# A pause in the token scatter at every fourth token tile

## The chip, the cores and the metric

One core of a Trainium2 chip runs the whole kernel. The metric is the device time of one execution in microseconds, as the median of the runs that were timed; smaller is better. The engines are named as the profile names them: PE is the matmul engine (PEld its weight loads), DVE the vector engine, ACT the scalar engine, POOL GpSimd, SP the engine that only issues transfers here.

## What is computed

The input is two sequences of 2048 tokens with 256 features. Both branches start from the layer-normed tokens. One is a spiking attention, the other a mixture of eight experts of which each token uses two. The reference, cut to this:

```python
xn = _layernorm(x)
# attention: Q, K, V are 0/1 spikes
Q = lif(layer_norm(query @ Wq.T + bq, gq, betaq), 1.0)      # K and V alike
hamming = q_sum + k_sum.T - 2.0 * qk
attn = Dh - hamming + log_pe_bias(N, N)
out = lif(einsum(attn * scale, V), 0.5)
out = lif(layer_norm(out @ Wo.T + bo, go, betao), 1.0)
# experts: each token goes to its two best of 8
scores, expert_idx = jax.lax.top_k(softmax(xt @ router_w.T), 2)
hidden = silu(h[..., :D]) * h[..., D:]                       # h = xt @ up_proj[e]
out_e = hidden @ down_proj[e]
result = x + attention + sum of the two out_e, weighted by gate
```

## The kernel before, in words

The 4096 tokens are 32 token tiles of 128. The normed tokens lie in SBUF as `xn`, 258 words a token: 256 features and two words that say where the expert result belongs. The program has these stages, in the order of time:

- **Start and routing** (0 to 65 us of the profile): load, norm, transposes, router logits, and on DVE the choice of experts. It ends with `pos`, two slot numbers for each token (semaphore `placed`, L901).
- **Scatter** (POOL, L677): `slot_x` is a DRAM buffer in which the tokens lie sorted by expert. For each of the 32 token tiles POOL issues two indirect transfers (TOPK = 2), each of which writes 128 rows of 1032 bytes to `slot_x`. That makes 64 transfers. Seven more (L684) write the empty slots; they are issued behind the tiles 3 to 6, two, two, two and one. POOL does not wait between them. Each of the 64 raises the semaphore `scattered` by 16 when it has landed.
- **Projection** (PE, ACT and DVE, beside the scatter): for each token tile PE computes Q, K and V. One tile is three groups of a bias matmul and six float32 matmuls (L1186, L1108 to L1110), and around them the transpose of an earlier tile's Q spikes (`turn_q`, L1174) and its K-V sum (`sum_kv`, L1195). ACT squares the results (`squares`, L500, waits for `proj_done`), moves Q (`keep_qT`, L488), and splits the next tile (`keep_xh`, L447); DVE makes the spikes (L960). The three engines hand tiles to each other in a short ring of buffers, so each is at most a few tiles ahead. Tiles 0 to 7 are written out, 8 to 19 are a loop, the rest is written out again. Tile 8 is the first of the loop; its project begins at 167.02 us in the profile, the last tile's ends at about 235 us.
- **Experts** (237 to 430 us): 71 slot tiles of 128 rows. SP reads them from `slot_x` (L353); before the first it waits for the whole scatter, for the seven others, and for the last expert weights that DVE splits. POOL writes each result with one indirect transfer to `slot_y` (L692).
- **Attention and output** (430 us to the end).

Who needs the scatter: SP's first read of `slot_x`, and nobody else. ACT waits at tile 11 for the seven other transfers (`pads_done`), since expert weights go where their rows lay.

Of the kernel before, what the change touches and what calls it, by code (L numbers as in the profile page):

```python
# [24 lines left out]
TOPK = 2  # L25
# [22 lines left out]
PAD_TILE = 3  # L48
LAG = 3
LATE = 11  # L50
FAR_ROWS = 5


# [4 lines left out]
def expert_blocks(a):  # L58

    n = [min(max(k - LAG, 0) * 4 // 3, NB) for k in (a, a + 1)]  # L60
    return range(*n)


def spiking_moe(nc, x, w_all, router, bias, gain, beta, scale, experts, ident, ident_b, toep, far_map, far_pick,
                head_mask, before, route_const, pad_mark, out):
    with ExitStack() as ctx:
        def sem(name):
            return ctx.enter_context(nc.semaphore(name))
# [177 lines left out]
        s = {n: sem(n) for n in names}  # L246
# [60 lines left out]
        def piece(n, h):  # L307
            return ew[:, n, h, :] if num(n) else ew[:, bass.ds(n, 1), h, :].rearrange("p a w -> p (a w)")

        def loop(eng, n, unroll, body, peel):  # L310

            for t in range(peel):
                body(t, t)
            with eng.Fori(0, (n - peel) // unroll) as i:
                for u in range(unroll):
                    body(i * unroll + (peel + u), peel + u)
# [8 lines left out]
        def _(sp):  # L325
# [57 lines left out]
            for a in range(NB):  # L383
                if a < LATE:
                    sp.wait_ge(s["fin_done"], a + 1)
                else:
                    sp.wait_ge(s["late_done"], a - LATE + 1)
                sp.dma_start(out_pairs[:, a], xres[:, a * B:(a + 1) * B, :]).then_inc(s["out_done"], 16)
# [237 lines left out]
        @block.gpsimd  # L626
        def _(pool):
            g = nc.gpsimd
            order = [0]

            def step(ins):
                order[0] += 1
                ins.then_inc(s["pool_order"], 1)

            def settled():
                pool.wait_ge(s["pool_order"], order[0])

            step(g.memset(neg_half[:, :], -0.5))
            g.memset(ones_b[:, :], 1.0).then_inc(s["ones_set"], 1)
            step(g.memset(pad_rows[:, :, :], 0.0))  # L640
            step(g.memset(ones_r[:, :].bitcast(F32), 1.0))
            step(g.memset(far_v[:, :], 0.0))
            g.memset(eps_c[:, :], EPS).then_inc(s["eps_set"], 1)
            step(g.memset(half_s[:, :], 0.0))
            step(g.memset(bias_r[:, :].bitcast(F32), 0.0))
            settled()
            step(g.memset(half_s[0:NB, :], -0.5))
            settled()

            pool.dma_start(pad_rows[:, :, D:ROW], pad_mark).then_inc(s["pads_marked"], 16)  # L650

            def first_rstd(c):
                pool.wait_ge(s["xvar_done"], c + 1)
                cols = slice(*X_CHUNKS[c])
                g.tensor_tensor(xrstd[:, cols], xvar[:, cols], neg_half[:, cols], ALU.pow).then_inc(s["xrstd_done"], 1)


            def piece_lower(n, m):
                pool.wait_ge(s["piece_h"], n + 1)
                g.tensor_tensor(piece(n, 1), ew_f[:, m % 2, :], piece(n, 0).bitcast(F32), ALU.subtract).then_inc(s["pool_piece"], 1)  # L660

            for c in range(len(X_CHUNKS) - 1):
                first_rstd(c)
            piece_lower(0, 0)
            first_rstd(len(X_CHUNKS) - 1)
            for n in range(1, POOL_PIECES):
                if n == 4:

                    pool.wait_ge(s["w_halved"], 2 * KC)
                    g.tensor_tensor(wo_l[:, :, :], w_f[:, :, G3 * D:], wo_h[:, :, :].bitcast(F32), ALU.subtract).then_inc(s["wo_parted"], 1)  # L670
                piece_lower(n, n)


            pool.wait_ge(s["placed"], 1)
            for t in range(NT):
                for k in range(TOPK):
                    pool.indirect_dma_start(slot_x, bass.IndirectOffsetOnAxis(ap=pos[:, k, t:t + 1], axis=0),  # L677
                                            xn[:, t, :], None).then_inc(s["scattered"], 16)
                if t == PAD_TILE:
                    pool.wait_ge(s["pads_placed"], 1)  # L680
                    pool.wait_ge(s["pads_marked"], 16)
                if t >= PAD_TILE:
                    for c in range(2 * (t - PAD_TILE), min(2 * (t - PAD_TILE) + 2, PC)):
                        pool.indirect_dma_start(slot_x, bass.IndirectOffsetOnAxis(ap=pad_i[:, c:c + 1], axis=0),  # L684
                                                pad_rows[:, c, :], None).then_inc(s["pads_done"], 16)


            def send(j, m):
                pool.wait_ge(s["dest_done"], j + 1)
                pool.wait_ge(s["ey_done"], j + 1)  # L690
                pool.sem_inc(s["sends_begun"], 1)
                pool.indirect_dma_start(slot_y, bass.IndirectOffsetOnAxis(ap=dest[:, m % 4:m % 4 + 1], axis=0),  # L692
                                        ey[:, m % 4, :], None).then_inc(y_out[m % 4], 16)
            loop(pool, 4 * QUADS, 4, send, peel=4)
            for j in range(4 * QUADS, SLOT_TILES):
                send(j, j)


            def out_rstd(a):
                pool.wait_ge(s["w_var"], a + 1)  # L700
                if a >= 2:
                    pool.wait_ge(s["w_spk"], B * (a - 1))
                g.tensor_tensor(rstd[:, a % 2, 0:B], veps[:, a % 2, 0:B], neg_half[:, 0:B], ALU.pow).then_inc(s["w_rstd"], 1)  # L703

            def add_spikes(a):

                if a == 0:
                    pool.wait_ge(s["xres_in"], 16 * NB)
                pool.wait_ge(s["w_spk"], B * (a + 1))
                both = xres[:, a * B:(a + 1) * B, :]  # L710
                g.tensor_tensor(both, both, spk[:, a, :, :], ALU.add).then_inc(s["spk_added"], 1)  # L711

            def finish(a):
                pool.wait_ge(s["moe_added"], B * (a + 1))
                if a < LATE:
                    pool.wait_ge(s["spk_added"], a + 1)
                both = xres[:, a * B:(a + 1) * B, :]
                g.tensor_tensor(both, both, y_tok[:, a, :, 0, :], ALU.add).then_inc(s["fin_done"], 1)  # L718

            for a in range(NB):  # L720
                out_rstd(a)
                if 1 <= a <= LATE:
                    add_spikes(a - 1)
                for e in expert_blocks(a - 1):
                    finish(e)
# [3 lines left out]
        def _(dve):  # L729
# [331 lines left out]
            def add_experts(a):  # L1061

                dve.wait_ge(s["gated"], B * (a + 1))
                for b in range(B):
                    v.scalar_tensor_tensor(y_tok[:, a, b, 0, :], y_tok[:, a, b, 0, :], gates[:, 0, a * B + b:a * B + b + 1],
                                           y_tok[:, a, b, 1, :], ALU.mult, ALU.add).then_inc(s["moe_added"], 1)
# [11 lines left out]
            def finish_late(a):  # L1078
                dve.wait_ge(s["w_spk"], B * (a + 1))
                dve.wait_ge(s["fin_done"], a + 1)  # L1080
                both = xres[:, a * B:(a + 1) * B, :]
                v.tensor_tensor(both, both, spk[:, a, :, :], ALU.add).then_inc(s["late_done"], 1)
# [3 lines left out]
            for a in range(NB + 2):  # L1086
# [4 lines left out]
                for e in expert_blocks(a - 2):  # L1091
                    add_experts(e)
                if a - 4 >= LATE:
                    finish_late(a - 4)
# [7 lines left out]
        def _(pe):  # L1102
# [120 lines left out]
            def experts_of(j, n):  # L1223

                _, es = nc.values_load_multi_w_load_instructions(
                    cut(owner[0:1, :], j, n), engines=[mybir.EngineType.PE], min_val=0, max_val=E - 1,
                    skip_runtime_bounds_check_because="a count of at most E - 1 experts' ends")
                return [ew[:, bass.ds(e * EP, EP), :, :] for e in es]
# [221 lines left out]
```

## Time and profile before

| what | value |
|---|---|
| timed runs | 511.02 us median of 3 (509.71 to 511.58) |
| span of the profiled execution | 510.6 us |
| PE busy | 384.5 us, 75% of the span |
| DVE, ACT, POOL busy | 273.3, 232.6, 211.0 us |
| mean granted PE clock | 0.883 of full speed |
| the 64 scatter instructions of POOL | 61.6 us busy, 65.5 to 155.2 us |

The span is that of the one execution that was profiled, on one core; it lies 0.4 us under the median of the timed runs. The times in the rows below are microseconds from the start of the span. The digits of the page's timeline are tenths busy in forty slices of 12.8 us each.

### The profile page before, as it was taken

The page shows a single profiled execution, that of the slowest core. Times are in us where ns is not written, and L with a number is a line of the kernel's source. Part 1 is how long each engine was busy: PE and PEld are TensorE (multiplying, and loading weights), DVE is VectorE, ACT ScalarE, POOL GpSimd, SP SyncE. Part 2 cuts the span into 40 slices and gives each one's busy share as a digit, 9 for nine tenths or more (in the row PEclk, how much of TensorE's full clock was granted, in tenths as well). Part 3 has the DMA queues.
Part 4 walks back from the last instruction along what each step waited for, and adds up shares of the span by engine and source line. Part 5 has one row for each costly group of instructions (what it writes and reads, how often), then busy time and mean ns, then how long its engine had stood idle before and what let it go on. Part 6 is the DMA issues. An engine that isn't in the chain of part 4 may idle for free.

```text
span 510.6 us, 9171 instructions
## 1 busy us (share of the span) xinstructions
PE 384.5 (75%) x2517; PEld 312.9 (61%) x2526; DVE 273.3 (54%) x774; ACT 232.6 (46%) x752; POOL 211.0 (41%) x213
## 2 busy tenths in 40 slices
PE   5498773110113999998999999999999999999960
PEld 2234662100112999997778888888888887667650
DVE  5799971000100687996545444554455442458995
ACT  1567421000001788986545544454445543366650
POOL 5242467777771000000233333333333333259993
PEclk9799985555555799999999999999999999999995
DMA  8721223222220111320443344343443332495222
GB/s 269 247 96 41 83 83 125 104 104 104 104 105 31 42 41 41 106 83 1 144 131 121 121 119 136 118 124 113 124 134 123 118 98 74 184 369 193 100 84 83
DMA packets 40432, 58.98 MB, mean 116 GB/s; under 512 B 6294, under 2 KB 27926, under 8 KB 40408
## 3 DMA queue, kind: packets, MB, share of 16 engines
q1 hardware_dynamic: 31712, 38.53, 24.5%
q0 software_dynamic: 6848, 18.70, 10.1%
q10 hardware_dynamic: 1848, 1.47, 0.9%
q8 instruction: 11, 0.18, 0.1%
q14 instruction: 13, 0.11, 0.1%
HBM read 35.79 MB, written 22.89 MB: 115 GB/s over the span
## 4 chain that ended last, share of the span: by engine, by line
PE 54%; issue 21%; DVE 10%; POOL 7%; DMA 3%; ACT 2%; SPq 1%; POOLq 0%; DVEq 0%; ACTq 0%
PE bank L1108 15%; PE bank L1109 14%; PE bank L1110 14%; POOL xres L718 3%; PE bank L1186 3%; PE bank L1251 3%; POOL xres L711 3%; PE bank L1235 3%; DMA xn<-x 2%; DVE xn L787 2%; DVE xst L765 2%; POOL rstd L703 1%; DVE w_f L808 1%; PE bank L1174 1%; PE bank L1195 1%
## 5 line engine op out<-in xcount | busy, mean ns | idle before, releaser
L692 POOL DMA_INDIRECT slot_y<-ey,dest x71 | 68.5, 965 | 214.6 <-ACT ey L554 186.2
L500 ACT ACTIVATE junk<-bank 128x256 bf16<-128x256 f32 x96 | 35.7, 379 | 89.8 <-remote 71.7
L677 POOL DMA_INDIRECT slot_x<-xn,pos x64 | 61.6, 963 | 23.9 <-issue 19.2
L996 DVE TENSOR_TENSOR hid<-gact,bank 128x256 f32<-128x256 f32 x71 | 29.9, 421 | 76.6 <-ACT gact L538 51.0
L1108 PE MATMUL bank<-ew,exT_h 128*128 x142 | 62.6, 441 | 5.6 <-issue 4.3
L1110 PE MATMUL bank<-w_h,xT_l 128*128 128x256 f32 x192 | 56.9, 296 | 11.3 <-issue 11.2
L795 DVE TENSOR_TENSOR xT_l<-xT,xT_h 128x256 fp32r<-128x256 f32 x28 | 12.9, 460 | 98.1 <-issue 54.1
L1109 PE MATMUL bank<-w_l,xT_h 128*128 128x256 f32 x192 | 56.9, 296 | 11.2 <-issue 11.2
L1108 PE MATMUL bank<-w_h,xT_h 128*128 128x256 f32 x192 | 57.1, 297 | 10.5 <-issue 10.4
L538 ACT ACTIVATE gact<-bank 128x256 f32<-128x256 f32 x71 | 27.4, 386 | 63.8 <-PE bank L1110 63.8
L1110 PE MATMUL bank<-ew,exT_l 128*128 x142 | 55.9, 394 | 0.0
L1109 PE MATMUL bank<-ew,exT_h 128*128 x142 | 55.9, 394 | 0.0
L1110 PEld LDWEIGHTS bank<-w_h,xT_l 128*128 128x128 f32 x192 | 39.6, 206 | 12.4 <-issue 12.4
L1109 PEld LDWEIGHTS bank<-w_l,xT_h 128*128 128x128 f32 x192 | 39.8, 207 | 12.0 <-issue 12.0
L1108 PEld LDWEIGHTS bank<-w_h,xT_h 128*128 128x128 f32 x192 | 39.9, 208 | 10.6 <-issue 10.6
L1108 PE MATMUL bank<-ew,hidT_h 128*128 x142 | 45.6, 321 | 1.0 <-DVE hidT_l L1000 1.0
L548 ACT ACTIVATE hidT_h<-bank 128x256 fp32r<-128x256 f32 x71 | 27.3, 385 | 33.1 <-issue 22.5
L1000 DVE TENSOR_TENSOR hidT_l<-bank,hidT_h 128x256 fp32r<-128x256 f32 x71 | 30.1, 425 | 21.3 <-ACT hidT_h L548 20.9
L1186 PE MATMUL bank<-bias_r,ones_r 128*128 128x256 f32 x96 | 31.4, 327 | 12.4 <-issue 8.5
L1109 PE MATMUL bank<-ew,hidT_h 128*128 x142 | 40.0, 282 | 0.0
L1110 PE MATMUL bank<-ew,hidT_l 128*128 x142 | 39.9, 281 | 0.0
L1108 PEld LDWEIGHTS bank<-ew,exT_h 128*128 128x128 f32 x142 | 26.7, 188 | 13.0 <-issue 10.0
(193 smaller groups left out, 967.9 us busy)
## 6 DMA issues: line engine op xcount, KB each, us to landing
ex<-slot_x SPq DMA_DIRECT2D x71, 129.0 KB
y_tok<-slot_y SPq DMA_DIRECT2D x8, 1024.0 KB, 13.6
ew_f<-experts SPq DMA_DIRECT2D x24, 256.0 KB, 2.6
xres<-x SPq DMA_DIRECT2D x16, 256.0 KB, 2.8
out<-xres SPq DMA_DIRECT2D x16, 256.0 KB, 2.1
xn<-x SPq DMA_DIRECT2D x6, 512.0 KB, 11.7
slot_y<-ey,dest POOLq DMA_INDIRECT x71, 2.8
xn<-x SPq DMA_DIRECT2D x4, 256.0 KB, 3.8
```

Source lines behind the costliest of these rows:

```text
L500: nc.scalar.activation(junk[:, i, :], proj_ps[r][i], ACT.Square, accum_out=ssq[:, r, i:i + 1]).then_inc(s["ssq_done"], 1)
L538: nc.scalar.activation(gact[:, m % 2, :], h_ps[m % 2][:, 0:F], ACT.Silu).then_inc(s["gact_done"], 1)
L548: nc.scalar.activation(flat2(hidT_h[:, m % 2, :, :]), hT_ps[m % 2], ACT.Copy).then_inc(s["hidh_set"], 1)
L677: pool.indirect_dma_start(slot_x, bass.IndirectOffsetOnAxis(ap=pos[:, k, t:t + 1], axis=0), xn[:, t, :], None).then_inc(s["scattered"], 16)
L692: pool.indirect_dma_start(slot_y, bass.IndirectOffsetOnAxis(ap=dest[:, m % 4:m % 4 + 1], axis=0), ey[:, m % 4, :], None).then_inc(y_out[m ...
L711: g.tensor_tensor(both, both, spk[:, a, :, :], ALU.add).then_inc(s["spk_added"], 1)
L996: v.tensor_tensor(hid[:, m % 2, :], gact[:, m % 2, :], h_ps[m % 2][:, F:2 * F], ALU.mult).then_inc(s["hid_done"], 1)
L1000: v.tensor_tensor(flat2(hidT_l[:, m % 2, :, :]), hT_ps[m % 2], flat2(hidT_h[:, m % 2, :, :]).bitcast(F32), ALU.subtract).then_inc(s["hidl_ ...
L1108: mm(dst, a_h, b_h, start=first, stop=False)
L1109: mm(dst, a_h, b_l, start=False, stop=False)
L1110: return mm(dst, a_l, b_h, start=False, stop=last)
L1186: mm(proj_ps[r][i], ones_r[:, :], bias_r[:, cols], start=True, stop=False)
```

## The change

In the scatter's loop POOL now waits, ahead of the token tiles 4, 8, 12, 16, 20, 24 and 28, until every scatter transfer issued so far has raised `scattered`, which it does on landing. Nothing is removed, and no transfer changes its size, its order or its issuer.

```diff
+BURST = 4
...
             pool.wait_ge(s["placed"], 1)
             for t in range(NT):
+                if t and t % BURST == 0:
+                    pool.wait_ge(s["scattered"], 16 * TOPK * t)
                 for k in range(TOPK):
                     pool.indirect_dma_start(slot_x, bass.IndirectOffsetOnAxis(ap=pos[:, k, t:t + 1], axis=0),
                                             xn[:, t, :], None).then_inc(s["scattered"], 16)
```

The program of POOL around the scatter, before: L677 is a scatter transfer, L684 one for the empty slots, and the number behind x counts equal ones.

```order
L677 DMA slot_x<-xn,pos 9088x258 [waits placed]
L677 DMA slot_x<-xn,pos 9088x258 x7
L684 DMA slot_x<-pad_rows,pad_i 9088x258 [waits pads_marked,pads_placed]
L684 DMA slot_x<-pad_rows,pad_i 9088x258
L677 DMA slot_x<-xn,pos 9088x258 x2
L684 DMA slot_x<-pad_rows,pad_i 9088x258 x2
```

The same place with the change, as far as the third pause. The lines have moved by three (L680, L687).

```order
L680 DMA slot_x<-xn,pos 9088x258 [waits placed]
L680 DMA slot_x<-xn,pos 9088x258 x7
L687 DMA slot_x<-pad_rows,pad_i 9088x258 [waits pads_marked,pads_placed]
L687 DMA slot_x<-pad_rows,pad_i 9088x258
L680 DMA slot_x<-xn,pos 9088x258 [waits scattered]
L680 DMA slot_x<-xn,pos 9088x258
L687 DMA slot_x<-pad_rows,pad_i 9088x258 x2
L680 DMA slot_x<-xn,pos 9088x258 x2
L687 DMA slot_x<-pad_rows,pad_i 9088x258 x2
L680 DMA slot_x<-xn,pos 9088x258 x2
L687 DMA slot_x<-pad_rows,pad_i 9088x258
L680 DMA slot_x<-xn,pos 9088x258 x2
```

No transfer has moved against another. The first pause stands behind the two transfers for empty slots that follow tile 3; each of the six later ones stands directly behind a scatter transfer.

## Rows read from the trace of the kernel before

**Rows 1.** The page: span, and busy tenths and GB/s in forty slices.

```profile
span 510.6 us, 9171 instructions
PE   5498773110113999998999999999999999999960
POOL 5242467777771000000233333333333333259993
PEclk9799985555555799999999999999999999999995
GB/s 269 247 96 41 83 83 125 104 104 104 104 105 31 42 41 41 106 83 1 144 131 121 121 119 136 118 124 113 124 134 123 118 98 74 184 369 193 100 84 83
```

**Rows 2.** Busy time by stretch: length, PE, PEld, DVE, ACT, POOL, clock, DMA share, GB/s.

```profile
65.40:165.40 100.00, 23.05 (x110) 18.44 (x109) 12.24 (x40) 7.19 (x29) 68.36 (x71) 0.55 0.27 97
167.00:235.00 68.00, 67.95 (x599) 66.50 (x600) 53.96 (x160) 55.20 (x220) 0.00 (x0) 0.96 0.21 59
```

**Rows 3.** Timeline of PE, 60 to 172 us: start, us, instruction, idle before it.

```profile
73.47 0.23 PE L1195 MATMUL bank<-v_spk,qk_spk 128*128 128x128 bf16 x1
...
105.73 0.37 PE L1110 MATMUL bank<-w_h,xT_l 128*128 128x256 f32 x1 [2.43 <-issue]
...
158.96 0.37 PE L1186 MATMUL bank<-bias_r,ones_r 128*128 128x256 f32 x1 [2.43 <-issue]
161.06 0.37 PE L1108 MATMUL bank<-w_h,xT_h 128*128 128x256 f32 x1 [1.73 <-issue]
...
163.17 0.57 PE L1108 MATMUL bank<-w_h,xT_h 128*128 128x256 f32 x1
...
165.27 0.37 PE L1110 MATMUL bank<-w_h,xT_l 128*128 128x256 f32 x1 [0.34 <-issue]
165.44 0.44 PE L1195 MATMUL bank<-v_spk,qk_spk 128*128 128x128 bf16 x2
```

**Rows 4.** Timeline of ACT, 55 to 180 us: four of its squares.

```profile
69.91 0.38 ACT L500 ACTIVATE junk<-bank 128x256 bf16<-128x256 f32 x1 [1.25 <-PE bank L1110]
...
88.22 0.38 ACT L500 ACTIVATE junk<-bank 128x256 bf16<-128x256 f32 x1 [7.99 <-remote]
...
123.97 0.38 ACT L500 ACTIVATE junk<-bank 128x256 bf16<-128x256 f32 x1 [34.91 <-remote]
...
164.63 0.39 ACT L500 ACTIVATE junk<-bank 128x256 bf16<-128x256 f32 x1 [28.77 <-remote]
```

**Rows 5.** Timeline of DVE and POOL: the scatter's release, its places around tile 4, its last.

```profile
64.98 0.20 DVE L901 CAST pos<-pos_f 128x64 int32<-128x64 f32 x1
...
65.46 1.06 POOL L677 DMA_INDIRECT slot_x<-xn,pos  x1 [4.70 <-DVE pos L901]
...
74.43 0.96 POOL L677 DMA_INDIRECT slot_x<-xn,pos  x1 [0.31 <-issue]
...
78.23 0.96 POOL L677 DMA_INDIRECT slot_x<-xn,pos  x1 [0.30 <-issue]
...
154.20 0.96 POOL L677 DMA_INDIRECT slot_x<-xn,pos  x1 [0.31 <-issue]
```

**Rows 6.** Busy time by stretch of 2 us, columns as in rows 2.

```profile
156.00:158.00 2.00, 0.37 (x1) 0.29 (x1) 0.00 (x0) 0.00 (x0) 0.00 (x0) 0.50 0.04 12
158.00:160.00 2.00, 0.37 (x1) 0.00 (x0) 0.00 (x0) 0.00 (x0) 0.00 (x0) 0.50 0.00 0
```

**Rows 7.** The page, DMA issues: KB each, median us from issue to landing.

```profile
slot_y<-ey,dest POOLq DMA_INDIRECT x71, 2.8
```

**Rows 8.** Timeline of SP's queue, 20 to 270 us: its first reads of slot_x.

```profile
225.61 24.14 SPq L353 DMA_DIRECT2D ex<-slot_x  x8
```

**Rows 9.** The expert stage: POOL's timeline, and busy time of one stretch.

```profile
270.48 0.96 POOL L692 DMA_INDIRECT slot_y<-ey,dest  x1 [1.59 <-ACT ey L554]
273.02 0.96 POOL L692 DMA_INDIRECT slot_y<-ey,dest  x1 [1.59 <-ACT ey L554]
...
270.00:300.00 30.00, 29.28 (x181) 25.10 (x179) 14.37 (x44) 14.53 (x45) 10.56 (x11) 1.00 0.40 123
```

## The prediction

> **What bounds the kernel now.** I read the page's slices first [rows 1]. PE is busy in nine tenths or more of nearly every slice from the 14th on, and it is almost idle in a hole of seven or eight slices, which are just those in which POOL's digit is 6 or 7 and the DMA rate stands at 104 GB/s: the scatter. So I read that hole by stretches [rows 2]. From 65.4 to 165.4 us PE has 110 matmuls and 23 us of work. From 167 to 235 us it has 599, is busy 67.95 of 68 us, and does the 24 token tiles 8 to 31, which is 68 / 24 = 2.83 us a tile. At that pace the 110 matmuls of the hole would take about 110 / 599 x 68 = 12.5 us. The hole costs the kernel some 87 us, and everything behind it simply starts later.
>
> What holds PE there? The timeline of PE [rows 3] runs without gaps until 73.47 us, 8 us into the scatter. After that a matmul comes every 2.1 to 2.8 us, with 2.43 us of idle time before it whose reason is given as "issue": no engine that the profile knows of is late. ACT's waits look like the cause but are not. Its squares [rows 4] wait 8, 35 and 29 us for "remote", and what they wait for in the code is `proj_done` of PE; the count for a tile whose matmuls are recorded by 73.5 us lets ACT go only at 123.97. So PE's completions are even later than its issues, and ACT and DVE wait behind PE. The scatter slows PE by something that is no semaphore of the program.
>
> The end of the hole matters most for this change. POOL issues its last scatter transfer at 154.20 us [rows 5]. DMA traffic is 12 GB/s in 156 to 158 us and nothing in 158 to 160 [rows 6], so it has landed by about 156.5. PE does not recover then. It still goes at the slow pace at 158.96, is a little quicker from 161.06 and runs freely only from 165.27 or 165.44 [rows 3]: **9 us after the last landing**, with no scatter traffic left.
>
> **The change part by part.** It adds seven waits on POOL. Nothing is removed. Behind the waiting instruction on POOL there are only more scatter transfers, those for the empty slots, and the expert stage's writes much later.
>
> - *The pause before tile 4.* Two transfers for empty slots (1.27 us each) stand between tile 3's last scatter transfer and the wait. That transfer starts at 74.43 and POOL reaches tile 4 at 78.23 [rows 5], 3.80 us later. Landing takes 2.8 us for the like transfer of the expert stage [rows 7]. The pause is over before it begins: 0 us.
> - *The six pauses before tiles 8 to 28.* Before, a transfer starts 1.27 us after the one before. Now it starts when the last has landed, and a wake-up later. No row gives the landing of a scatter transfer, so I bound it: at the short end 156.5 - 154.2 = 2.3 us by the traffic's end [rows 5, 6], at the long end 2.8 us from the like transfer [rows 7]. The wake-up is 0.28 us, from DVE's end at 64.98 + 0.20 = 65.18 to POOL's start at 65.46 [rows 5]. The extra time per pause is then 2.3 + 0.28 - 1.27 = 1.3 us to 2.8 + 0.28 - 1.27 = 1.8 us. The transfers are of one kind and size with those of rows 7 but for 8 bytes in a row, and the landing counts only when the slowest sixteenth is in, so I lean to the upper end and take 1.6 us. Six of them are **9.6 us** (7.8 to 10.8).
>
> The Trainium skill (DMA: Bandwidth & Descriptors, section Anatomy of one DMA) gives such a transfer a fixed 2.0 us plus its bytes at 436 GB/s. For 132 KB that is, as an estimate from the page, 2.3 us, and the six pauses would come to 7.9 us. Rows 7 say more, and the sum above stays with them.
>
> *Is the scatter's end on the path?* Its reader is not: SP first reads `slot_x` at 225.61 [rows 8], 69 us after the last landing. But the hole that the scatter makes is on the path with its whole length, since PE is fully busy afterwards [rows 2]. If the slow pace lasts as long as the scatter and 9 us more, the hole ends 9.6 us later. In those 9.6 us PE does at most what it does in the hole, 110 matmuls in 100 us, so some 10 matmuls, which are worth 10 / 599 x 68 = 1.2 us. The sum is +9.6 - 1.2 = **+8.4 us**.
>
> *Does a pause let PE go?* This is the unknown term. A pause leaves about 1.3 to 1.8 us without new traffic, and what follows is a new burst of eight transfers, 8 x 1.27 = 10.1 us. After the last transfer PE needed 9 us of silence to recover, and for the first 4.5 of them (156.5 to 161.06) it did not quicken at all [rows 3]. A pause is much shorter than that, so I take the relief as nothing. The bound on the other side comes from the scatter's start: there PE ran freely for 8 us (65.46 to 73.47) [rows 3, 5]. Were each pause a full reset, each of six bursts would give 8 us of free work.
>
> Everything after the hole keeps its order and its durations, so it only shifts. PE's clock, at 0.5 from the seventh slice to the thirteenth [rows 1], rises after the hole as before.
>
> The profiled execution would go from 510.6 to 519.0 us. The median of the timed runs lies 0.4 us above that span, so I say **519.5 us**.
>
> **The rivals.**
>
> *The pause opens as much free time as it costs.* PE is free while no transfer is in flight, slow otherwise. Then each pause gives back its own 1.6 us in work at full pace. For it: the hole and the scatter's traffic coincide at the front. Against it: the 9 us at the end. The sum is 9.6 - 6 x 1.6 = 0, and the time 511 us.
>
> *The other side: the pause resets what holds PE.* The hold is then a backlog that builds up over some microseconds of unbroken issue; PE slows only 8 us after the first transfer, while in the expert stage, where the same kind of transfer comes every 2.5 us instead of 1.27, PE is busy 29.28 of 30 us [rows 9]. So the rate matters, and somewhere between these two rates the hold goes away. The pauses lower the rate from one per 1.27 us to eight per 11.7 us, one per 1.46. Where after each pause PE runs at full pace for 4 us, half of what the start shows, it gains 6 x 4 = 24 us and the time is 511 + 9.6 - 24 = 497 us; with the full 8 us it is 473. It decides from 1.6 us of free work per pause. Against it stands again the end: what takes 9 us to clear does not clear in 1.6 unless it is much smaller after ten microseconds of scatter than after ninety.
>
> The Trainium skill (NOTIFIC — the notification-queue block, section 7.1, Overflow) describes one such backlog: a block of the core whose internal queues, when full, stall the engines that feed them. No run here shows it. By that rule the chances would lean to this rival, for queues drain when the inflow stops; yet the 9 us at the scatter's end would be the time for draining them, and by it a pause of 1.6 us would drain a fifth.
>
> *Longer pauses.* If POOL's wait is held up in the way PE is (its own wake-up late by the 1.4 us that PE spends on an instruction, half of 2.8), the pauses cost 6 x 1.4 = 8.4 us more: 528 us. For the scatter's reader to become the bound, a pause would have to last 69 / 6 = 11.5 us; I see nothing that would make it so.
>
> *The waits do nothing* (all has landed each time): not possible for the six, since POOL would reach the wait about 1 us after the last issue and no row shows a landing below 2 us.
>
> **How the numbers follow.** No relief, forecast: 0.56, with 516 to 523 us. Longer pauses 0.04, around 528. Equal 0.13, around 511. Reset 0.27, around 497 with a wide spread, 475 to 508. The range of 494 to 526 us takes in the forecast, the equal case and a good half of the reset, and leaves out the deep end of the reset (0.13) and longer pauses (0.05). The likeliest case's own range is 516 to 523. The chances of faster, same and slower, with 0.5% (2.6 us) as about what a measurement of this kernel can tell, are 0.27, 0.13 and 0.60.
>
> **What would show it.** In the profile of the changed kernel POOL should have six gaps of 1.3 to 1.8 us more than the usual 0.30 in front of L680, none at tile 4, and its last scatter instruction should start near 163.8 us. PE should crawl from 74 us until about 174 us without a free stretch, and tile 8's first matmul should come at about 175 us instead of 167.02. I am wrong if PE shows dense runs of matmuls right after the pauses, if tile 8 starts before 167 us, or if the gaps on POOL are several microseconds long.

## The result and the profile after

The changed kernel takes 496.68 us (median of 4, 495.99 to 497.31) against 511.23 us for the kernel before (median of 4). The ratio is 0.9712, with a 95% interval of 0.9685 to 0.9738: it is faster by 2.9%, where 519.5 us was forecast. The profiled execution has a span of 494.2 us, 16.4 us less than before. Every 95% interval here and below compares only runs that lie within 1.5% of the fastest run of their kernel.

The page of the changed kernel, span and busy tenths in forty slices (12.4 us each here):

```profile
span 494.2 us, 9179 instructions
PE   4588784232666799989999999999999999999960
POOL 5252457666666200001333333333333333269993
PEclk9799886555567899999999999999999999999995
```

The hole of [rows 1] has filled in part: in the slices 8 to 13 PE's digits are 2 to 6, where most of them were 0 or 1. The hundred microseconds from 65.4 us in the changed kernel, columns as in [rows 2]:

```profile
65.40:165.40 100.00, 47.67 (x238) 39.21 (x238) 23.66 (x74) 20.39 (x79) 68.17 (x71) 0.62 0.31 103
```

PE issues 238 matmuls in them instead of 110 [rows 2]. POOL's timeline in the changed kernel, around the first pause that finds something in flight, the last such pause and the scatter's end (start, us, instruction, idle before it):

```profile
93.21 0.96 POOL L680 DMA_INDIRECT slot_x<-xn,pos  x1 [0.30 <-issue]
96.22 0.96 POOL L680 DMA_INDIRECT slot_x<-xn,pos  x1 [2.04 <-DMA slot_x<-xn,pos]
...
155.03 0.96 POOL L680 DMA_INDIRECT slot_x<-xn,pos  x1 [2.12 <-DMA slot_x<-xn,pos]
...
163.88 0.96 POOL L680 DMA_INDIRECT slot_x<-xn,pos  x1 [0.30 <-issue]
```

There are six such gaps; start to start they last 2.70 to 3.08 us, 1.66 us more than the usual 1.27 on average. Between the tiles 3 and 4 there is none. PE's timeline in the changed kernel behind the pause that ends at 119.45, and around the last landing:

```profile
115.91 0.27 PE L1198 MATMUL bank<-v_spk,qk_spk 128*128 128x128 bf16 x1 [1.20 <-issue]
121.99 0.39 PE L1177 MATMUL bank<-id_b,qk_spk 128*128 128x128 bf16 x2 [5.82 <-issue]
123.14 0.58 PE L1189 MATMUL bank<-bias_r,ones_r 128*128 128x256 f32 x1 [0.76 <-issue]
123.52 0.41 PE L1111 MATMUL bank<-w_h,xT_h 128*128 128x256 f32 x1
...
161.87 0.28 PE L1198 MATMUL bank<-v_spk,qk_spk 128*128 x2
164.19 0.27 PE L1177 MATMUL bank<-id_b,qk_spk 128*128 128x128 bf16 x2 [2.04 <-issue]
165.18 0.38 PE L1189 MATMUL bank<-bias_r,ones_r 128*128 128x256 f32 x1 [0.71 <-DVE xT_l L798]
```

At 123.14 tile 8 begins, 3.7 us behind POOL's restart. Its first 14 matmuls follow one another without a gap, for 3 us; then there are two gaps of 1.0 us. The tiles 9 and 10 begin at 134.87 and 145.60, again 3.5 and 2.5 us behind a restart: about one tile per pause, where in the kernel before two tiles took the 86 us from 80.71 to 167.02 us. At 165.18, with the last transfer just issued, tile 13 begins. Before, tile 8 began at 167.02.

One thing must be said ahead of the experiments. They ran in six further series, each with its own runs of the kernel before. In three of these PE is held during the scatter, and the kernel before takes 511.7 to 512.3 us, as in the first series. In the other three it is not held at all, and the same kernel takes 438.9 to 439.9 us. Within a series it never changed. What sets it I do not know. The record numbers the chips: the series without the hold ran on the chips 0, 5 and 5, those with it on 5, 9 and 12, and the first series has no number. Number 5 stands on both sides, so the number alone does not decide it, and the words "The chips differ" in an expectation below are not borne out.

### The profile page after: what moved, and what is told of

Its sections match the earlier page's. It is cut to its first block, busy times and chain, and to the rows that moved or that the text cites. A ratio compares the mean times of both kernels' runs of the same rounds, so it can differ in the third digit from the quotient of the medians.

```text
span 494.2 us, 9179 instructions
## 1 busy us (share of the span) xinstructions
PE 394.8 (80%) x2525; PEld 319.2 (65%) x2526; DVE 274.3 (56%) x774; ACT 233.2 (47%) x752; POOL 211.0 (43%) x213
## 3 DMA queue, kind: packets, MB, share of 16 engines
q0 software_dynamic: 6848, 18.70, 10.4%
## 4 chain that ended last, share of the span: by engine, by line
PE 55%; issue 15%; DVE 10%; POOL 8%; another core or an unknown queue 3%; DMA 3%; ACT 3%; SPq 1%; DVEq 0%; POOLq 0%; ACTq 0%
PE bank L1111 15%; PE bank L1112 14%; PE bank L1113 14%; POOL xres L721 3%; PE bank L1254 3%; POOL xres L714 3%; PE bank L1238 3%; PE bank L1189 3%; DMA xn<-x 2%; DVE xn L790 2%; DVE xst L768 2%; POOL rstd L706 1%; ACT junk L501 1%; DVE w_f L811 1%
## 5 line engine op out<-in xcount | busy, mean ns | idle before, releaser
L680 POOL DMA_INDIRECT slot_x<-xn,pos x64 | 61.7, 964 | 33.8 <-issue 17.4
L1111 PE MATMUL bank<-w_h,xT_h 128*128 128x256 f32 x192 | 59.4, 309 | 7.9 <-issue 7.7
L1112 PE MATMUL bank<-w_l,xT_h 128*128 128x256 f32 x192 | 59.5, 310 | 5.9 <-issue 5.8
L1113 PE MATMUL bank<-w_h,xT_l 128*128 128x256 f32 x192 | 59.8, 312 | 4.2 <-issue 4.2
L1112 PEld LDWEIGHTS bank<-w_l,xT_h 128*128 128x128 f32 x192 | 42.2, 220 | 8.7 <-issue 8.7
L1113 PEld LDWEIGHTS bank<-w_h,xT_l 128*128 128x128 f32 x192 | 42.0, 219 | 6.9 <-issue 6.9
L1111 PEld LDWEIGHTS bank<-w_h,xT_h 128*128 128x128 f32 x192 | 42.5, 222 | 5.6 <-issue 5.6
L1189 PE MATMUL bank<-bias_r,ones_r 128*128 128x256 f32 x96 | 33.0, 343 | 8.6 <-DVE xT_l L798 5.3
## 6 DMA issues: line engine op xcount, KB each, us to landing
xn<-x SPq DMA_DIRECT2D x6, 512.0 KB, 11.5
```

Source lines behind the costliest of these rows:

```text
L1111: mm(dst, a_h, b_h, start=first, stop=False)
L1112: mm(dst, a_h, b_l, start=False, stop=False)
L1113: return mm(dst, a_l, b_h, start=False, stop=last)
L1189: mm(proj_ps[r][i], ones_r[:, :], bias_r[:, cols], start=True, stop=False)
```

## The experiments

**Four edits, first series without the hold.** The burst is halved and doubled (`BURST = 2`, `BURST = 8`). Or the wait gives way to work of the same length that waits for no landing:

```diff
-                if t and t % BURST == 0:
-                    pool.wait_ge(s["scattered"], 16 * TOPK * t)
+                if t >= 2 * BURST and t % BURST == 0:
+                    step(g.tensor_tensor(gates[:, 0, 0:8], ones_r[:, 0:8].bitcast(F32), neg_half[:, 0:8], ALU.pow))
+                    settled()
```

Or the same mean pace without pauses:

```diff
                 for k in range(TOPK):
+                    if t or k:
+                        step(g.memset(gates[:, :, :], 0.0))
+                        settled()
```

> Pauses at every second token tile: 15 waits, of which 13 find a transfer in flight and cost about 1.66 us each (the mean of the six in the changed kernel), 22 us in all. Theory A (what holds PE is a backlog that grows while transfers are issued without a break, and a pause clears it): bursts of four transfers last 5.1 us, less than the 8 us that PE ran freely at the scatter's start, so PE is hardly held; the projection ends before 180 us and the time falls well below 480 us. Theory B (each pause gives a fixed 4 us of free work): 511 + 22 - 13 x 4 = 481 us. Theory C (a pause gives back what it costs and no more, the gain of the changed kernel has another source): 497 to 511 us.

> Pauses at every eighth token tile: three waits, 5 us in all. Theory A: a burst of sixteen transfers lasts 20 us, of which PE is held for the larger part, as in the kernel before; 503 to 508 us. Theory B: 511 + 5 - 3 x 4 = 504 us. Theory C: about 511 us.

> The wait for the landings is taken out; in its place POOL computes a small power (8 columns into a tile that is not yet in use) at the six places, about 1.8 us, so that the gap in the issue is as long but no landing is waited for. Theory A: the same relief, 494 to 500 us. Theory D (it is the landing of every transfer that lets PE go, not the gap): 511 us or up to 10 us more.

> No pauses: POOL sets a small unused tile ahead of each scatter transfer, so each transfer is 0.2 to 0.35 us later, 12 to 22 us over the scatter, as much as or more than the six pauses together, but in 63 small pieces. Theory A in the form that a real break is needed: 511 to 530 us, since the backlog never clears. Theory E (only the mean rate of transfers counts): as fast as the changed kernel or faster, 480 to 497 us.

Measured: 465.57, 446.13, 449.40 and 448.02 us, against 439.18 us for the kernel before, where all four expectations stood on 511. None of the theories was tested: there was no hold to relieve (PE issues 712 to 719 matmuls from 65.4 to 165.4 us in the four traces), and each edit cost about what it added to the scatter.

**Both kernels again.**

> The kernel before once more, unchanged, for its trace in this series: here it took 439.2 us beside the first four experiments, 72 us less than the 511 of the first runs. Theory F (the hole of PE is no property of the kernel but comes and goes with where or when it runs): either about 439 us with tile 8 of the projection near 80 us and no crawl of PE, or about 511 us with tile 8 near 167 us; nothing between. Theory G (the hole was there in the four experiments as well and something else was shorter): PE crawls from 74 us here too.

> The changed kernel once more, unchanged, timed against the one before on the same chip. Theory F, where the hole is absent: the scatter's end is itself on the path, the six pauses come through whole, 439.2 + 6 x 1.66 = 449.2 us, slower by 2.3%; where it is present: 497 us against 511, faster by 2.9%. Theory G: 0.971 of the kernel before, whatever that takes.

In this series PE was held again: 512.10 us for the kernel before (512.33 as the median of its seven other runs), 496.75 us for the changed one, ratio 0.9639 (0.9595 to 0.9684). The hole is back, which both theories allow. What rules G out is the traces of the first four edits, with their 712 to 719 matmuls: the hole comes and goes as a whole, as theory F has it. The ratio 0.9639 is without the longest of the four runs, 503.59 us; the medians of all runs give 0.970, close to the first 0.9712. The four runs spread from 492.63 to 503.59 us, where the first four lay between 495.99 and 497.31, so the size of the relief varies.

**Two of the edits where PE is held, and two new ones.** In the first new one POOL waits for the projection instead of for landings:

```diff
-                if t and t % BURST == 0:
-                    pool.wait_ge(s["scattered"], 16 * TOPK * t)
+                if t:
+                    pool.wait_ge(s["proj_done"], G3 * t)
```

The second is the kernel before with shorter rows (`H = D // 2 + 2`), here two of its places. It leaves out half of each token's features, in the scatter and in SP's reads, and the experts compute on the first half twice, so its result is not the reference's; it serves for its time alone:

```diff
-        slot_x = nc.dram_tensor("slot_x", (SLOTS, ROW), F32, kind="Internal").ap()
+        slot_x = nc.dram_tensor("slot_x", (SLOTS, H), F32, kind="Internal").ap()
...
-                                            xn[:, t, :], None).then_inc(s["scattered"], 16)
+                                            xn[:, t, 0:H], None).then_inc(s["scattered"], 16)
```

> Pauses at every second token tile once more. The chips differ: on one the kernel before takes 439 us and shows no hole, on another 512. Where the hole is present, theory A (a backlog that a pause clears): about 470 us, since bursts of four transfers are too short to hold PE, and the projection is done before the scatter, whose end at about 180 us is then the bound as in the first run of this edit (465.6 us). Theory B (a fixed 4 us of free work per pause): 481 to 485 us. Where it is absent: 465 us against 439.

> The same gap in the issue, without a wait for landings, once more. Where the hole is present, theory A: 492 to 500 us, as the changed kernel; theory D (only the wait for the landing of all transfers lets PE go): 512 to 522 us. Where it is absent: 449 us against 439.

> No wait for landings: ahead of token tile t POOL waits until PE has finished the projection of the tiles before t, so the scatter can never run ahead of the projection. Where the hole is absent the projection is ahead of the scatter nearly everywhere: 439 to 442 us. Where it is present, theory A: POOL stops by itself whenever PE is held, and goes on when PE has moved, so that the hold clears each time; 450 to 490 us. Theory H (the hold, once there, persists as long as transfers come at all): 505 us or more, with the scatter stretched out to the projection's end.

> The kernel before with rows of 130 words instead of 258 in the scatter, in slot_x and in its reads: the same transfers, rows and completions, half the bytes (the experts then compute on the first 128 features twice). Theory I (the bytes written are what holds PE): the hole shrinks to less than half, 440 to 475 us where the kernel before takes 512. Theory J (the number of transfers or of their rows and completions holds PE): 505 to 515 us, less a few us for the shorter reads. Where the hole is absent: within 2 us of 439.

Measured, against 511.96 us: 463.45 us (0.9052, 0.9013 to 0.9091), 491.40 us (two runs, 487.26 and 495.54, too far apart for a ratio, but both at least 16 us under the kernel before), 453.46 us (0.8857, 0.8838 to 0.8876) and 511.23 us (0.9987, 0.9967 to 1.0008). So the landings are not needed (theory D is out), a pause is not worth a fixed 4 us (theory B asked for 481 to 485 us with a pause at every second tile), the hold does not last as long as transfers come (theory H is out), and half the bytes change nothing (theory I is out). The software queue's packets went down too, from 6848 to 5712:

```profile
q0 software_dynamic: 5712, 14.05, 7.8%
```

The paced scatter does best. PE and POOL from 85 to 155 us in the execution with short rows, then in that with the pace:

```profile
85.00:155.00 70.00, 9.82 (x30) 7.37 (x30) 2.19 (x8) 1.83 (x7) 53.25 (x56) 0.50 0.16 53
```

```profile
85.00:155.00 70.00, 59.63 (x496) 56.27 (x496) 45.26 (x133) 47.30 (x189) 45.95 (x45) 0.91 0.41 129
```

With 56 transfers in 70 us PE gets 30 matmuls done, with 45 transfers 496. How the pace works shows in its POOL timeline:

```profile
104.33 0.96 POOL L680 DMA_INDIRECT slot_x<-xn,pos  x1 [0.90 <-PE bank L1113]
105.60 0.96 POOL L680 DMA_INDIRECT slot_x<-xn,pos  x1 [0.30 <-issue]
107.41 0.96 POOL L680 DMA_INDIRECT slot_x<-xn,pos  x1 [0.85 <-PE bank L1113]
```

From 96 us on it adds about half a microsecond per tile, and PE runs nearly without a break. Before that, while PE is still held, POOL stops for 1.78 and 1.69 us, ahead of its transfers at 89.87 and 95.06. The scatter ends late here (last start 170.13 us), and SP's first read follows at 172.68, 12.6 us later than in the kernel before without the hold (160.12): most of what is left between 453.5 and 439 us.

**The pace and the spread scatter, without the hold.**

> The small piece of work ahead of each transfer once more, where the chip allows: one transfer per 1.42 to 1.46 us without any pause, which is the mean rate of the changed kernel (eight per 11.8 us, one per 1.47). Where the hole is present, theory E (the mean rate counts): about 490 to 500 us, as with six pauses. Theory A in the form that a real break is needed: 515 to 522 us, PE crawling from 74 us until 9 us after the scatter. Where it is absent: 448 us against 439.

> The scatter paced by the projection, once more: 453.5 us on a chip on which the kernel before takes 512. Where the hole is present again: 451 to 456 us. Where it is absent: the projection is ahead of the scatter until near its end, so 439 to 444 us against 439; a loss of more than 10 us would mean that the waits on PE's tiles stretch the scatter there too.

Measured, against 438.94 us: spread 447.70 us; pace 438.71 us (ratio 0.9988, 0.9963 to 1.0013), no change.

**Both kernels side by side without the hold.**

> As before for this edit: where the hole is present, 490 to 500 us if the mean rate of the transfers counts, 515 to 522 us if a real break is needed; where it is absent, 448 us.

> Three pauses. Where the hole is present, theory A with what the changed kernel showed (a pause frees about one further token tile, 2.8 us, and costs 1.66 us; six pauses gave five tiles and 14.5 us): three pauses give 5 to 8 us, 504 to 507 us against 512. If the hold grows with the length of a burst, less than that, 508 to 512 us. Where it is absent: 446 us.

> The changed kernel. Where the hole is present: 493 to 499 us, faster. Where it is absent: the scatter's end is on the path and each of the six pauses costs what the gap costs, 439 + 10 = 449 us, slower by 2.3%.

> The kernel before, for its trace beside the third run of the changed one. Where the hole is absent: 439 us, tile 8 of the projection near 79 us, and SP's first read of slot_x directly behind the last landing, at about 158 us. Where it is present: 512 us, tile 8 near 168 us.

Measured, against 439.85 us: spread 447.93, three pauses 445.25, the changed kernel 451.18 us (1.0229, 1.0167 to 1.0290), the kernel before 439.53. The first two again say nothing on the hold. The last two show the other side of the change. The hundred microseconds of [rows 2] in this execution of the kernel before:

```profile
65.40:165.40 100.00, 84.92 (x726) 81.04 (x726) 69.00 (x209) 67.13 (x263) 71.73 (x71) 0.93 0.43 137
```

PE has 726 matmuls there instead of 110. The projection is done by about 155 us, and the path is now the scatter itself; the chain that ended last, in this execution:

```profile
157.50 2.60 DMA slot_x<-xn,pos
160.12 2.06 DMA ex<-slot_x
```

In the changed kernel of the same series one pause was longer than any in the first, and SP's first read came at 172.75 us instead of 160.12, which is all of the difference in span (450.4 against 437.7 us):

```profile
136.21 0.96 POOL L680 DMA_INDIRECT slot_x<-xn,pos  x1 [3.01 <-DMA slot_x<-xn,pos]
```

```profile
172.75 16.94 SPq L354 DMA_DIRECT2D ex<-slot_x  x8
```

**Breaks or mean pace, at last where PE is held.**

> As before for this edit: where the hole is present, 490 to 500 us if the mean rate of the transfers counts, 515 to 522 us if a real break is needed; where it is absent, 448 us.

> As before for this edit: where the hole is present, 504 to 507 us if a pause is worth the same however long the burst, 508 to 512 us if a longer burst leaves a larger hold; where it is absent, 445 us.

Measured, against 511.70 us: the spread scatter 499.58 us (two runs, 496.70 and 502.45; ratio 0.977, 0.9636 to 0.9905), the three pauses 510.47 us (0.9967, 0.9941 to 0.9993). So without one break the spread scatter gives most of what six pauses gave, and three breaks give next to nothing, as expected for the case that a longer burst leaves a larger hold (508 to 512 us). The theory that a real break is needed asked for 515 to 522 us and has fallen: both runs lie below the kernel before. The expected 490 to 500 us held one of them. From 85 to 155 us in the spread scatter, in the one with three pauses, and in the changed kernel:

```profile
85.00:155.00 70.00, 36.11 (x132) 27.14 (x130) 11.04 (x34) 12.07 (x47) 56.00 (x98) 0.52 0.30 105
```

```profile
85.00:155.00 70.00, 15.80 (x49) 11.56 (x50) 4.40 (x13) 4.71 (x18) 49.27 (x51) 0.50 0.29 100
```

```profile
85.00:155.00 70.00, 27.90 (x111) 21.95 (x112) 9.64 (x31) 11.54 (x45) 45.47 (x48) 0.55 0.29 98
```

All executions with the hold, by the mean interval between POOL's 71 transfers (first start to last start, over 70):

| kernel | mean interval, us | matmuls, 85 to 155 us | time, us |
|---|---|---|---|
| before | 1.27 | 28 | 511.2 |
| short rows | 1.27 | 30 | 511.2 |
| three pauses | 1.35 | 49 | 510.5 |
| changed kernel | 1.41 | 111 | 496.7 |
| spread | 1.42 | 132 | 499.6 |
| six gaps, no wait | 1.43 | 139 | 491.4 |
| paced by PE | 1.50 | 496 | 453.5 |
| pause at every second tile | 1.67 | 361 | 463.5 |

The times are medians, the other columns are of the profiled execution of each. Between 1.41 and 1.43 the order means little: a second profile of the changed kernel has 152 matmuls at an interval of 1.44 us. Down to the row of the six gaps PE's share grows steeply with a small slackening of the scatter. The row paced by PE is to be read otherwise: there POOL follows PE, so the interval is as much a result of PE's speed as its cause, and that a fixed interval of 1.50 us would free PE is not shown. In the last row PE was held early, until about 107 us, and the scatter ends so late (last start 181.84 us) that it is the bound again.

The table holds only where PE is held. In the trace of the kernel before without the hold the interval is 1.32 us, and PE has 559 matmuls from 85 to 155 us. What makes the difference between the two conditions is therefore not the pace of the scatter.

## Why the prediction was wrong, step by step

- **Where the time lies: right.** The hole was the part that moved. What lies behind it kept its length: SP's first read of `slot_x` came at 209.20 instead of 225.61 us, 16.4 us earlier, and the span is 16.4 us shorter (the medians of the timed runs differ by 14.5 us).
- **The picture of the hold: incomplete.** "After that a matmul comes every 2.1 to 2.8 us" leaves out short dense stretches, at 80.71 and at 136.37 us, and above all that PE also stands still, for 24 us at one place:

```profile
135.70 0.37 PE L1174 MATMUL bank<-id_b,qk_spk 128*128 128x128 bf16 x2 [24.11 <-issue]
```

  It goes on 0.15 us after ACT's copy of Q (L488, 135.17 to 135.55 us), and ACT had been let go late, at 123.97 [rows 4]. In the changed kernel the longest gap of this kind is 7.31 us. The crawl itself has steps: from 91 us on the matmuls of the kernel before start mostly 2.80 or 2.10 us apart, those of the changed kernel, where they crawl, mostly 1.40 or 0.70. The hold is thus a matter of degree, and the prediction took it as one fixed speed.
- **The price of the pauses: right.** Forecast 0 us at tile 4 and six times 1.6 us, 9.6 in all; measured none and six times 1.66, 9.9. The landing with its wake-up is 2.70 to 3.08 us; less the 0.28 us of [rows 5] the landing alone is 2.4 to 2.8 us, 2.65 on average. By the Trainium skill (DMA: Bandwidth & Descriptors, section Anatomy of one DMA) the estimate was 2.3 us, somewhat too short; rows 7 were nearer. (Longer pauses stand in the prediction once with 0.04 and once with 0.05, which changes nothing here.)
- **The relief: wrong, and this is the step that failed.** "A pause is much shorter than that, so I take the relief as nothing" read the 9 us of silence at the scatter's end as the time that any relief needs. That time is not fixed. In the changed kernel there is no such tail: the last transfer starts at 163.88 us, and tile 13 runs densely from 165.18, before that transfer can have landed. With three pauses the last burst is 20 us long and its last transfer starts at 159.15 us, which puts its landing at 161.8 by the mean of 2.65; PE is free some 3 us later:

```profile
163.01 0.37 PE L1111 MATMUL bank<-w_h,xT_h 128*128 128x256 f32 x1 [1.03 <-issue]
164.41 0.37 PE L1112 MATMUL bank<-w_l,xT_h 128*128 128x256 f32 x1 [1.02 <-issue]
164.58 0.41 PE L1113 MATMUL bank<-w_h,xT_l 128*128 128x256 f32 x1
```

  Read so, the 9 us were the time to work off what ninety microseconds of unbroken issue had left, not what a pause has to last to help. In the runs the extra time of 1.66 us a pause bought (14.5 + 9.9) / 6 = 4.1 us of free work.
- **The rival that came true** was the one on the other side, with 4 us per pause and 497 us, to which I gave 0.27. Its size came out right in part by luck: 4 us was half of what the scatter's start showed, and with three pauses, which cost 5.3 us together and left 1.2 us of gain, each bought only (1.2 + 5.3) / 3 = 2.2 us. Its reason, a reset by the pause, was only half right: the spread scatter has no pauses and gains nearly as much. Its other sentence, that the rate matters and that between 1.27 and 2.5 us per transfer the hold goes away, is what the runs bear out in its direction: from 1.27 to 1.43 us the hold weakens, and paced by PE it is gone from about 95 us on. At which fixed interval it goes away was not run.
- **What I should have seen:** a PE that in the hole gets 110 matmuls [rows 2], and is dense on both sides of it, may be living on what is left over. If the scatter takes nearly all of something, a tenth less of it multiplies the remainder: the cost of a pause then counts in tenths of the scatter, its gain in multiples of that remainder. The table fits this picture; no run shows what the something is. I worked out the 1.2 us of extra crawl at the old crawl speed, as if it would stay.
- **What stays open:** what PE is held by. It is not the bytes and not the wait for landings, and it is absent in three of the seven series. The Trainium skill (NOTIFIC — the notification-queue block, section 7.1, Overflow) describes internal queues that stall their producers when full. A backlog that fills within 8 us, drains within 9 and relaxes as the inflow slackens behaves like that; no run shows that it is such a queue. Nor can the runs tell whether the recording of the events takes part: each of them has its own recorded span and clock, so there is none without. Finer transfers, which would have told the count of transfers from the count of rows, and plain transfers in place of indirect ones were not tried on the chip.

## What to carry to other kernels

When an engine crawls for no reason that its semaphores give, look at what another engine issues without a break, and pace that by the progress of the engine that suffers, not by a fixed pause: here the paced scatter took 453.5 us where the kernel before took 512.0 and the changed one 496.7, and cost nothing where PE was not held (438.7 against 438.9). A fixed pause is a bet: it won about 3% in one condition and lost 2.3% in the other, because there the scatter's end was the path. And a recovery time read at the end of a long load says little about a short pause within it: here it was 9 us behind ninety microseconds of scatter, and 3 us behind twenty.

## What the hardware showed that I had not expected

The same program takes 439 or 512 us, the same in every run of a series and different from one series to the next, with a PE that issues 726 or 110 matmuls in the same hundred microseconds. The clock takes part in it: in the hole the granted clock is 0.50 (1.2 GHz), in the execution without the hold it is 0.93 on average over that stretch, mostly 2.4 GHz; but with 0.37 us of PE work in some 2.8 us of crawl a slower clock cannot be what fills the rest. In the crawl PE waits for nothing that the profile names, ACT and DVE follow behind it, and POOL, whose stream of transfers it hangs on, keeps its mean of 1.27 us. Without the hold POOL is even a little slower, at 1.32 us.
